# Layernorm scales from a power on GpSimd in place of a square root on ScalarE and a reciprocal on VectorE

## The chip, the cores and the metric

One core of one Trainium2 chip runs the whole kernel in one launch. The metric is device microseconds from the start to the end of the program; less is better. The engines are named as in the profile: PE (TensorE matmul), DVE (VectorE), ACT (ScalarE), POOL (GpSimd), SP (SyncE, which only issues DMAs).

## The reference

The reference is a small transformer of four layers with several kinds of attention and of mixture-of-experts blocks, on 2048 rows (8 x 256) of 256 columns in float32. Each block takes a layernorm of the running sum x and adds its result to x. Cut to what matters:

```python
def _layernorm(x, axis=-1, eps=1e-05):
    m = jnp.mean(x, axis=axis, keepdims=True)
    v = jnp.var(x, axis=axis, keepdims=True)
    return (x - m) / jnp.sqrt(v + eps)

x = x + 0.5 * L0_ffn(_layernorm(x))
x = x + L0_attn(_layernorm(x))
x = x + 0.5 * L0_ffn(_layernorm(x))
x = x + 0.5 * L1_ffn(_layernorm(x))
x = x + L1_attn(_layernorm(x))     # x + its own result; starts with an rms norm
x = x + 0.5 * L1_ffn(_layernorm(x))
x = x + 0.5 * L2_ffn(_layernorm(x))
x = x + L2_attn(_layernorm(x))
x = x + 0.5 * L2_ffn(_layernorm(x))
x = x + 0.5 * L3_ffn(_layernorm(x))
x = x + L3_attn(_layernorm(x))
x = x + 0.5 * L3_ffn(_layernorm(x))
```

Each ffn routes every row to two experts and adds shared experts that every row passes.

## The kernel before

The 2048 rows are 16 tiles (NT) of 128 partitions. x stays on the chip in X (16 tiles of 128x256). The program is a list of thirteen stages, numbered from 0: ffn L0, attn0, ffn L0, moe L1, attn1, ffn AFT (the second half of attn1), moe L1, moe L2, attn2, moe L2, moe L3, attn3, moe L3. Each engine walks through all stages with a program of its own, in the order in which it is written; semaphores join them.

All stages but AFT begin with a layernorm, the "front". It works in four groups of four tiles (GROUP = 4), g = 0 to 3. For each group:

1. DVE takes the moments (front_moments): four bn_stats (L597), four bn_aggr (L600) into MV (mean and variance of each row), and VE = variance + eps (L602). attn1 needs a second scale, since it follows the layernorm with an rms norm: L604 makes its VE, so its tiles are 128x8 instead of 128x4.
2. ACT takes the square root, SD (front_root, L610).
3. DVE takes RS = 1 / SD (L621) and the shift NB = -mean * RS (L622), in front_deviations; attn1 has four operations there (L616 to L619).
4. ACT applies scale and shift, one 128x256 ACTIVATE a tile (front_norm, L631), into XN or XNR. For a moe stage it also issues a DMA that stores the rows to DRAM (front_store, L637), for the experts' gathers.
5. PE transposes the rows (L717), ACT copies the high halves XTH (L723) and DVE takes the low halves XTL (L729): each float32 operand is split into two parts for PE.

In eight stages (0 to 3, 6, 9, 11, 12) the front stands by itself at the start of the stage. In the other four (attn1, the first L2, attn2 and the first L3, stages 4, 7, 8 and 10) it is "tailed": it runs within the tail of the moe stage before it.

The tail of a moe stage brings the experts' results back. POOL issues, tile after tile, two indirect DMAs (the gathers, L1736), one for each of a row's two experts, into YG, whose buffers hold four tiles: the gathers of tile t wait until tile t - 4 is done (x_done). DVE's combines (L1599 and L1604) wait for them and add the weighted rows to X. ACT, PE and DVE go through the tail in numbered slots k: in the slot m.front_of(g) DVE takes the moments of group g, and the square root, the norm, the transposes and the splits of that group follow in this slot and the next three. Tiles 6 and 7 are combined just before the moments of group 0 in an L1 tail, tiles 14 and 15 just before those of group 3.

POOL has other work besides the gathers. At the start of a stage that has weights to split into high and low parts, it casts and subtracts them piece by piece: L2943 and L2945 for the ffn stages and the projections of attn1 and attn3, L1704 and L1706 for the moe stages, L2071 to L2088 for attn0. In a moe stage it also takes some of the shared experts' low halves (SHL, L1573) and issues the gathers of the experts' rows (L1724). Stages 6, 9 and 12 load weights that the program has kept in DRAM from an earlier stage.

PE takes a product with split operands as three matmuls, at L546, L547 and L548. The routing of the ffn and moe stages is a chain of small DVE operations on 128x112 or 128x128 (L756 to L763 for L0).

Of the kernel before, what the change touches and what calls it, by code (L numbers as in the profile page):

```python
# [10 lines left out]
ALU = mybir.AluOpType  # L11
# [151 lines left out]
def build(nc, d, out):  # L163

    with ExitStack() as ctx:
# [44 lines left out]
        M128 = main.put('M128', [P, NT])  # L210
        RST = main.put('RST', [P, 16, NT])
        W12 = main.put('W12', [P, 2, NT])
        SGT = main.put('SGT', [P, NT])
# [353 lines left out]
        def tables_vector(dve):  # L567
# [7 lines left out]
            nc.vector.tensor_copy(HALVES[:, :], MCR[0:32, 3 * P + 2 * NT + 16 * NT:])  # L575
            nc.vector.memset(SEVEN[:, :], 7)
            for m in MOES.values():
                nc.vector.memset(SIZES[:, 2 * m.router:2 * m.router + 1], float(m.ecols))
                nc.vector.memset(SIZES[:, 2 * m.router + 1:2 * m.router + 2], float(m.base))
            nc.vector.memset(RWS[:, :, :, 48:64].bitcast(F32), 0.0)  # L580
            nc.vector.tensor_copy(RWS[:, :, :, 0:16], RWR[:, :, :, :]).then_inc(consts, 1)
            dve.wait_ge(consts, 3)
            nc.vector.tensor_copy(RWS[:, :, :, 32:48], RWR[:, :, :, :])
# [6 lines left out]
        def front_moments(dve, st, g):  # L590
# [8 lines left out]
            for t in tiles:  # L599
                last = nc.vector.bn_aggr(MV[:, t, :], ST6[:, t, :])  # L600
            step(last)
            last = nc.vector.tensor_scalar(VE[:, part], MV[:, part, 1], LN_EPS, None, ALU.add)  # L602
            if st.kind == 'attn1':
                last = nc.vector.tensor_scalar(twice(VE)[:, 1, part], MV[:, part, 1], 1.0 + AFT_EPS, AFT_EPS * LN_EPS, ALU.mult, ALU.add)  # L604
            last.then_inc(ln_var, 1)

        def front_root(act, st, g):
            act.wait_ge(ln_var, GROUPS * st.ln + g + 1)
            sets = slice(0, 1 + (st.kind == 'attn1'))
            nc.scalar.activation(twice(SD)[:, sets, tiles_of(g)[1]], twice(VE)[:, sets, tiles_of(g)[1]], ACT.Sqrt).then_inc(ln_sd, 1)  # L610

        def front_deviations(dve, st, g):
            part = tiles_of(g)[1]
            dve.wait_ge(ln_sd, GROUPS * st.ln + g + 1)
            if st.kind == 'attn1':
                step(nc.vector.reciprocal(twice(RS)[:, :, part], twice(SD)[:, :, part]))  # L616
                step(nc.vector.scalar_tensor_tensor(NB[:, part], MV[:, part, 0], -1.0, twice(RS)[:, 1, part], ALU.mult, ALU.mult))
                nc.vector.scalar_tensor_tensor(MV[:, part, 0], MV[:, part, 0], -1.0, RS[:, part], ALU.mult, ALU.mult)
                nc.vector.tensor_scalar(MV[:, part, 1], RS[:, part], 1.0, None, ALU.add).then_inc(ln_rs, 1)  # L619
                return  # L620
            step(nc.vector.reciprocal(RS[:, part], SD[:, part]))  # L621
            nc.vector.scalar_tensor_tensor(NB[:, part], MV[:, part, 0], -1.0, RS[:, part], ALU.mult, ALU.mult).then_inc(ln_rs, 1)  # L622

# [30 lines left out]
        def front_vector(dve, st):  # L654
            for g in range(GROUPS + 2):
                if g < GROUPS:
                    front_moments(dve, st, g)
                if g == 0 and not st.xd:
                    tables_vector(dve)
                if g >= 2:  # L660
                    front_low(dve, st, 2 * g - 4)
                    front_low(dve, st, 2 * g - 3)
                if g < GROUPS:
                    front_deviations(dve, st, g)
                if g == 1 and st.kind == 'attn0':
                    attn0_prepare(dve, st)

        def front_scalar(act, st):
            for g in range(GROUPS + 2):
                if g < GROUPS:  # L670
                    front_root(act, st, g)
                if 1 <= g < GROUPS + 1:
# [15 lines left out]
        def front_tensor(pe, st):  # L688
            pe.wait_ge(consts, 4)
            for g in range(GROUPS + 2):  # L690
# [700 lines left out]
        def moe_scalar(act, st):  # L1391
# [46 lines left out]
            for k in range(m.front_of(GROUPS - 1) + (4 if nx else 1)):  # L1438
                if k < m.late:
                    shared_scalar(act, st, m.early + k)  # L1440
                for g in range(GROUPS if nx else 0):
# [7 lines left out]
                    if k == done + 1:  # L1449
                        front_norm(act, nx, g)  # L1450
                        if nx.kind == 'moe':
                            front_store(act, nx, g)
                    if k == done:
                        front_root(act, nx, g)
                if nx and nx.kind == 'attn2':
# [150 lines left out]
        def moe_vector(dve, st):  # L1606
# [63 lines left out]
            for k in range(m.front_of(GROUPS - 1) + (3 if nx else 1)):  # L1670
# [3 lines left out]
                for g in range(GROUPS if nx else 0):  # L1674
                    done = m.front_of(g)
                    if k == done + 1:
                        front_deviations(dve, nx, g)
                    if k == done + 2:
# [30 lines left out]
        def moe_pool(pool, st):  # L1709
# [21 lines left out]
            for t in range(NT):  # L1731
                if t >= YGS // 2:
                    pool.wait_ge(x_done, st.xd + t - YGS // 2 + 1)
                for c in range(2):
                    i = 2 * (NT * st.moe + t) + c
                    nc.gpsimd.indirect_dma_start(YG[:, i % YGS, :], None, dyo[0:m.blocks * P, :],  # L1736
                                                 bass.IndirectOffsetOnAxis(ap=POSI[:, c * NT + t:c * NT + t + 1], axis=0)
                                                 ).then_inc(y_in[i // 2 % (YGS // 2)], 16)

        def moe_sync(sp, st):  # L1740
# [324 lines left out]
        def attn0_pool(pool, st):  # L2065
# [15 lines left out]

            rounds = st.pieces // PIECES
            for q in range(PIECES):
                pool.wait_ge(raw_in[q], 16 * (rounds + 1))
                nc.gpsimd.tensor_copy(HWH[:, 0, q * PIECE:(q + 1) * PIECE], RAW[:, q, 0:PIECE]).then_inc(w_hi, 1)
                if q < 2:
                    tap_sums(0, q, 2 * q)
                piece_lo(0, q, st.pieces + q + 1)  # L2088
# [859 lines left out]
        def _(pool):  # L2948
            for st in stages:
                if st.xd and st.kind != 'attn2':  # L2950
                    pool.wait_ge(x_done, st.xd)
                if st.kind == 'moe':
                    moe_pool(pool, st)
# [193 lines left out]
```

## Time and profile before

| | |
|---|---|
| median of three runs | 3247.46 us |
| lowest and highest | 3237.97 and 3249.4 us |
| profiled execution: span, first to last instruction | 3310.2 us |
| PE, DVE, ACT, POOL busy in it | 87%, 67%, 45%, 47% |
| mean clock granted to PE | 0.924 of full |

The profile is of one execution. The only time of its own that it shows is the span, which is 62.7 us above the median of the runs shown. Shares of busy time are means over thirteen stages with different limits: what a change in one place is worth is read from the timeline of that place.

### The profile page before, as it was taken

To read this page: it belongs to the slowest core of one execution; us is meant where nothing else is said; L and a number is where in the kernel's file an instruction comes from. 1 tells how busy PE (TensorE), PEld (TensorE's weight loads), DVE (VectorE), ACT (ScalarE), POOL (GpSimd) and SP (SyncE) were. 2 spreads that over 40 slices of the span, in tenths; PEclk is the share of its full clock that TensorE was granted. 3 is DMA by queue.
4 is the path that set the end of the run, shared out by engine and by line. 5 is a ranking of instruction groups with operands and counts; after the bars stand their busy time and mean duration, and the time that the engine had idled before them with its cause. 6 is when DMAs were issued, how large, how long until landed. Compare 5 with 4: busy or idle time off the path is not lost. (4 is left out here: it accounts for less than half of the span.)

```text
span 3310.2 us, 60075 instructions
## 1 busy us (share of the span) xinstructions
PE 2869.5 (87%) x20922; PEld 2560.7 (77%) x20922; DVE 2213.8 (67%) x5794; ACT 1489.4 (45%) x3235; POOL 1556.3 (47%) x1511
## 2 busy tenths in 40 slices
PE   8979999999999899886897967579997858977798
PEld 6869999999999787774686947557776746956697
DVE  6767777777777677765636656478886555654655
ACT  3356565666566524335323443345444334433342
POOL 2345556555555216444401346658882547350143
PEclk9989999999999898997899977879997869988899
DMA  4022122212121302361005434600003442550533
GB/s 149 1 74 68 53 71 55 71 55 71 55 71 55 114 1 79 103 223 34 20 0 191 122 96 151 205 8 2 2 2 140 118 128 81 193 185 1 204 104 98
DMA packets 147763, 285.78 MB, mean 86 GB/s; under 512 B 20673, under 2 KB 70209, under 8 KB 144385
## 3 DMA queue, kind: packets, MB, share of 16 engines
q1 hardware_dynamic: 113458, 211.38, 19.3%
q0 software_dynamic: 21216, 57.96, 6.6%
q10 hardware_dynamic: 12816, 12.78, 1.1%
q8 instruction: 174, 2.85, 0.4%
q14 instruction: 99, 0.81, 0.1%
HBM read 191.59 MB, written 90.45 MB: 85 GB/s over the span
## 5 line engine op out<-in xcount | busy, mean ns | idle before, releaser
L1724 POOL DMA_INDIRECT MXG<-dxn,IDX x250 | 237.3, 949 | 233.9 <-PE bank L1281 174.3
L1736 POOL DMA_INDIRECT YG<-dyo,POSI x192 | 187.6, 977 | 212.7 <-DMA dyo<-YS 107.7
L2688 POOL TENSOR_SCALAR SX<-SX,MN 128x256 f32<-128x256 f32 x256 | 233.7, 929 | 46.0 <-DVE MN L2619 45.9
L1573 POOL TENSOR_TENSOR SHL<-SGS,SHH 128x512 fp32r<-128x512 f32 x36 | 49.0, 1362 | 425.0 <-ACT SHH L1375 422.8
L2619 DVE CUSTOM_DVE_ANT_0 SX<-bank,FMASK 128x128 f32<-128x128 f32 (+1 forms) x512 | 156.1, 351 | 48.1 <-PE bank L2532 48.0
L1098 POOL TENSOR_TENSOR HL<-HID,HH 128x512 fp32r<-128x512 f32 x56 | 72.4, 1292 | 241.7 <-ACT HH L1063 241.5
L546 PE MATMUL bank<-MWH,GH 128*128 x500 | 171.9, 344 | 13.2 <-DVE HB L1644 6.6
L1411 ACT ACTIVATE GH<-bank 128x256 fp32r<-128x256 f32 x250 | 96.5, 387 | 179.5 <-PE bank L1281 173.6
L546 PE MATMUL bank<-MWH,SHH 128*128 128x256 f32 x352 | 111.7, 317 | 73.6 <-POOL SHL L1573 26.5
L548 PE MATMUL bank<-MWH,GL 128*128 x500 | 156.1, 312 | 0.0
L547 PE MATMUL bank<-MWL,GH 128*128 x500 | 156.0, 312 | 0.0
L1639 DVE TENSOR_TENSOR GL<-bank,GH 128x256 fp32r<-128x256 f32 x250 | 105.5, 423 | 70.9 <-ACT GH L1411 54.1
L2591 ACT ACTIVATE PT<-bank 128x384 f32<-128x384 f32 x256 | 111.7, 490 | 79.9 <-PE bank L2541 79.5
L1988 DVE TENSOR_TENSOR VL<-bank,VH 128x512 fp32r<-128x512 f32 x128 | 82.4, 686 | 96.1 <-ACT VH L1941 96.1
L546 PE MATMUL bank<-MH,XTH 128*128 128x256 f32 x512 | 145.0, 283 | 1.1 <-DVE ML L2036 1.1
L547 PE MATMUL bank<-ML,XTH 128*128 128x256 f32 x512 | 144.9, 283 | 0.0
L548 PE MATMUL bank<-MH,XTL 128*128 128x256 f32 x512 | 144.8, 283 | 0.0
L1418 ACT ACTIVATE HB<-bank 128x176 f32<-128x176 f32 (+1 forms) x250 | 75.7, 303 | 149.3 <-PE bank L548 106.6
L2079 POOL TENSOR_TENSOR HWL<-RAW,HWH 128x640 fp32r<-128x640 f32 x68 | 115.1, 1702 | 56.6 <-DVE DEC L1984 56.4
L546 PEld LDWEIGHTS bank<-MWH,SHH 128*128 128x128 f32 x352 | 73.1, 208 | 88.0 <-issue 30.6
L546 PE MATMUL bank<-MWH,HTH 88*128 (+1 forms) x406 | 136.9, 337 | 1.6 <-DVE HTL L1648 0.9
L546 PE MATMUL bank<-XTH,MWH 128*128 128x512 f32 x320 | 134.4, 420 | 3.8 <-POOL MWL L1706 3.4
(465 smaller groups left out, 11634.0 us busy)
## 6 DMA issues: line engine op xcount, KB each, us to landing
dyo<-YS SPq DMA_DIRECT2D x250, 128.0 KB
RAW<-in_wheads SPq DMA_DIRECT2D x68, 320.0 KB
BB<-dgates SPq DMA_DIRECT2D x68, 256.0 KB, 3.6
GB<-dgates SPq DMA_DIRECT2D x68, 256.0 KB, 4.2
RAW<-in_eL SPq DMA_DIRECT2D x32, 304.0 KB
dkeptL<-MWL SPq DMA_DIRECT2D x32, 304.0 KB
dkeptL<-MWH SPq DMA_DIRECT2D x32, 304.0 KB
MWH<-dkeptL SPq DMA_DIRECT2D x8, 1216.0 KB, 13.3
```

The source lines that it names most:

```text
L546: nc.tensor.matmul(o, lh, rh, start=start, stop=False)
L547: nc.tensor.matmul(o, lh, rl, start=False, stop=False)
L548: return nc.tensor.matmul(o, ll, rh, start=False, stop=stop)
L1411: nc.scalar.activation(GH[:, b % DEEP, :], bank[X_BANK[b % 2]][:, 0:D], ACT.Copy).then_inc(b_xhi, 1)
L1639: nc.vector.tensor_tensor(GL[:, b % DEEP, :], bank[X_BANK[b % 2]][:, 0:D], f32(GH[:, b % DEEP, :]), ALU.subtract).then_inc(b_xlo, 1)
L1724: nc.gpsimd.indirect_dma_start(MXG[:, n % XGS, :], None, dxn, bass.IndirectOffsetOnAxis(ap=IDX[:, b:b + 1], axis=0)).then_inc(x_in[n % XGS ...
L1736: nc.gpsimd.indirect_dma_start(YG[:, i % YGS, :], None, dyo[0:m.blocks * P, :], bass.IndirectOffsetOnAxis(ap=POSI[:, c * NT + t:c * NT + t ...
L1988: return nc.vector.tensor_tensor(VL[:, s % 2, 2 * o:2 * o + 2, :], bank[4 + o][:, :].rearrange('p (t d) -> p t d', t=2), f32(VH[:, s % 2, ...
L2079: nc.gpsimd.tensor_tensor(HWL[:, parity, part], RAW[:, slot, 0:PIECE], f32(HWH[:, parity, part]), ALU.subtract).then_inc(w_ready, 1)
L2591: nc.scalar.activation(PT[:, n % RING3, :], bank[TURNED_IN[n % 2]][:, 0:TRI], ACT.Exp, scale=-1.0).then_inc(s_exp, 1)
L2619: last = nc.vector.tensor_tensor_reduce(out=SX[:, n % RING2, part], in0=o[:, part], in1=FMASK[:, part], scale=-float(HD) ** -0.5, scalar=3 ...
L2688: nc.gpsimd.tensor_scalar(part, part, MN[:, n % RING2, 1:2], None, ALU.subtract).then_inc(s_less1, 1)
```

## The change

The square root on ACT and the reciprocal and products on DVE go. POOL takes one operation for both, a power of VE with the exponent -0.5 out of a new constant tile, MINUS, and then the shift NB as a product with the mean, whose sign DVE now turns in front_moments (one more operation a group). For attn1 POOL takes the four operations. Between the power and the product POOL waits for its own semaphore.

Where POOL does this differs. In the fronts that stand by themselves all four groups come at the start of the stage, before POOL's weight splits; in attn0 the root of group g + 1 stands ahead of piece g of the weights. In the tailed fronts the roots stand in the loop of the gathers: group 0 behind the gathers of tile 7, group 1 behind those of tile 11, groups 2 and 3 behind those of tile 15.

The memset of MINUS raises the semaphore of the constants once more, so the waits on it go from 3 and 4 to 4 and 5, and the roots of stage 0 wait for it too.

```diff
@@ -209,6 +209,7 @@
         IDH = main.put('IDH', [P, NT], F16)
         M128 = main.put('M128', [P, NT])
         RST = main.put('RST', [P, 16, NT])
+        MINUS = main.put('MINUS', [P, 2 * NT])
         W12 = main.put('W12', [P, 2, NT])
         SGT = main.put('SGT', [P, NT])
         POSI = main.put('POSI', [P, 2 * NT], I32)
@@ -574,12 +575,13 @@
             nc.vector.memset(ONE16[:, :], 1.0)
             nc.vector.tensor_copy(HALVES[:, :], MCR[0:32, 3 * P + 2 * NT + 16 * NT:])
             nc.vector.memset(SEVEN[:, :], 7)
+            nc.vector.memset(MINUS[:, :], -0.5).then_inc(consts, 1)
             for m in MOES.values():
                 nc.vector.memset(SIZES[:, 2 * m.router:2 * m.router + 1], float(m.ecols))
                 nc.vector.memset(SIZES[:, 2 * m.router + 1:2 * m.router + 2], float(m.base))
             nc.vector.memset(RWS[:, :, :, 48:64].bitcast(F32), 0.0)
             nc.vector.tensor_copy(RWS[:, :, :, 0:16], RWR[:, :, :, :]).then_inc(consts, 1)
-            dve.wait_ge(consts, 3)
+            dve.wait_ge(consts, 4)
             nc.vector.tensor_copy(RWS[:, :, :, 32:48], RWR[:, :, :, :])
             nc.vector.tensor_tensor(RWS[:, :, :, 16:32], RWR[:, :, :, :], f32(RWS[:, :, :, 0:16]), ALU.subtract).then_inc(consts, 1)
 
@@ -599,27 +601,30 @@
             for t in tiles:
                 last = nc.vector.bn_aggr(MV[:, t, :], ST6[:, t, :])
             step(last)
+            nc.vector.tensor_scalar(MV[:, part, 0], MV[:, part, 0], -1.0, None, ALU.mult)
             last = nc.vector.tensor_scalar(VE[:, part], MV[:, part, 1], LN_EPS, None, ALU.add)
             if st.kind == 'attn1':
                 last = nc.vector.tensor_scalar(twice(VE)[:, 1, part], MV[:, part, 1], 1.0 + AFT_EPS, AFT_EPS * LN_EPS, ALU.mult, ALU.add)
             last.then_inc(ln_var, 1)
 
-        def front_root(act, st, g):
-            act.wait_ge(ln_var, GROUPS * st.ln + g + 1)
+        def front_root(pool, st, g):
+            part = tiles_of(g)[1]
             sets = slice(0, 1 + (st.kind == 'attn1'))
-            nc.scalar.activation(twice(SD)[:, sets, tiles_of(g)[1]], twice(VE)[:, sets, tiles_of(g)[1]], ACT.Sqrt).then_inc(ln_sd, 1)
-
-        def front_deviations(dve, st, g):
-            part = tiles_of(g)[1]
-            dve.wait_ge(ln_sd, GROUPS * st.ln + g + 1)
+            if not st.xd:
+                pool.wait_ge(consts, 5)
+            pool.wait_ge(ln_var, GROUPS * st.ln + g + 1)
+            nc.gpsimd.tensor_tensor(twice(RS)[:, sets, part], twice(VE)[:, sets, part], twice(MINUS)[:, sets, part], ALU.pow).then_inc(ln_sd, 1)
+            pool.wait_ge(ln_sd, GROUPS * st.ln + g + 1)
             if st.kind == 'attn1':
-                step(nc.vector.reciprocal(twice(RS)[:, :, part], twice(SD)[:, :, part]))
-                step(nc.vector.scalar_tensor_tensor(NB[:, part], MV[:, part, 0], -1.0, twice(RS)[:, 1, part], ALU.mult, ALU.mult))
-                nc.vector.scalar_tensor_tensor(MV[:, part, 0], MV[:, part, 0], -1.0, RS[:, part], ALU.mult, ALU.mult)
-                nc.vector.tensor_scalar(MV[:, part, 1], RS[:, part], 1.0, None, ALU.add).then_inc(ln_rs, 1)
+                nc.gpsimd.tensor_tensor(NB[:, part], MV[:, part, 0], twice(RS)[:, 1, part], ALU.mult)
+                nc.gpsimd.tensor_tensor(MV[:, part, 0], MV[:, part, 0], RS[:, part], ALU.mult)
+                nc.gpsimd.tensor_scalar(MV[:, part, 1], RS[:, part], 1.0, None, ALU.add).then_inc(ln_rs, 1)
                 return
-            step(nc.vector.reciprocal(RS[:, part], SD[:, part]))
-            nc.vector.scalar_tensor_tensor(NB[:, part], MV[:, part, 0], -1.0, RS[:, part], ALU.mult, ALU.mult).then_inc(ln_rs, 1)
+            nc.gpsimd.tensor_tensor(NB[:, part], MV[:, part, 0], RS[:, part], ALU.mult).then_inc(ln_rs, 1)
+
+        def front_roots(pool, st):
+            for g in range(GROUPS):
+                front_root(pool, st, g)
 
         def front_norm(act, st, g):
             act.wait_ge(ln_rs, GROUPS * st.ln + g + 1)
@@ -660,15 +665,11 @@
                 if g >= 2:
                     front_low(dve, st, 2 * g - 4)
                     front_low(dve, st, 2 * g - 3)
-                if g < GROUPS:
-                    front_deviations(dve, st, g)
                 if g == 1 and st.kind == 'attn0':
                     attn0_prepare(dve, st)
 
         def front_scalar(act, st):
             for g in range(GROUPS + 2):
-                if g < GROUPS:
-                    front_root(act, st, g)
                 if 1 <= g < GROUPS + 1:
                     front_high(act, st, 2 * g - 2)
                     front_high(act, st, 2 * g - 1)
@@ -686,7 +687,7 @@
                 nc.tensor.matmul(bank[b][:, 0:2 * P], TRB[:, 0, :], TRB[:, :, :].rearrange('p c t -> p (c t)'), start=True, stop=True)
 
         def front_tensor(pe, st):
-            pe.wait_ge(consts, 4)
+            pe.wait_ge(consts, 5)
             for g in range(GROUPS + 2):
                 if st.routed and 2 <= g < GROUPS:
                     moe_logits(pe, st, 2 * g - 4)
@@ -1450,8 +1451,6 @@
                         front_norm(act, nx, g)
                         if nx.kind == 'moe':
                             front_store(act, nx, g)
-                    if k == done:
-                        front_root(act, nx, g)
                 if nx and nx.kind == 'attn2':
                     if k == m.late + 1:
                         act.wait_ge(shared_added, st.added + NW)
@@ -1673,8 +1672,6 @@
                     shared_product(dve, st, m.early + k)
                 for g in range(GROUPS if nx else 0):
                     done = m.front_of(g)
-                    if k == done + 1:
-                        front_deviations(dve, nx, g)
                     if k == done + 2:
                         front_low(dve, nx, 2 * g)
                         front_low(dve, nx, 2 * g + 1)
@@ -1736,6 +1733,9 @@
                     nc.gpsimd.indirect_dma_start(YG[:, i % YGS, :], None, dyo[0:m.blocks * P, :],
                                                  bass.IndirectOffsetOnAxis(ap=POSI[:, c * NT + t:c * NT + t + 1], axis=0)
                                                  ).then_inc(y_in[i // 2 % (YGS // 2)], 16)
+                for g in range(GROUPS if st.next else 0):
+                    if t == min(GROUP * g + GROUP - 1 + YGS // 2, NT - 1):
+                        front_root(pool, st.next, g)
 
         def moe_sync(sp, st):
             m = st.m
@@ -2080,7 +2080,10 @@
                                         ALU.subtract).then_inc(w_ready, 1)
 
             rounds = st.pieces // PIECES
+            front_root(pool, st, 0)
             for q in range(PIECES):
+                if q + 1 < GROUPS:
+                    front_root(pool, st, q + 1)
                 pool.wait_ge(raw_in[q], 16 * (rounds + 1))
                 nc.gpsimd.tensor_copy(HWH[:, 0, q * PIECE:(q + 1) * PIECE], RAW[:, q, 0:PIECE]).then_inc(w_hi, 1)
                 if q < 2:
@@ -2949,6 +2952,8 @@
             for st in stages:
                 if st.xd and st.kind != 'attn2':
                     pool.wait_ge(x_done, st.xd)
+                if st.name != 'AFT' and st.kind != 'attn0' and not st.tailed:
+                    front_roots(pool, st)
                 if st.kind == 'moe':
                     moe_pool(pool, st)
                 if st.kind == 'attn0':
```

## Rows read from the trace of the kernel before

**Rows 1.** The page: busy time of each engine.
```profile
PE 2869.5 (87%) x20922; PEld 2560.7 (77%) x20922; DVE 2213.8 (67%) x5794; ACT 1489.4 (45%) x3235; POOL 1556.3 (47%) x1511
```

**Rows 2.** Groups by line, ACT's and DVE's: count, busy us, mean ns, idle us before, releaser.
```profile
L631 ACT ACTIVATE XN<-X,NB,RS 128x256 f32<-128x256 f32 x128 | 66.2, 590 | 9.3 <-DVE NB L622 9.3
...
L610 ACT ACT_TABLE_LOAD x11 | 14.1, 1283 | 0.9 <-PEq L3139 0.7
...
L610 ACT ACTIVATE SD<-VE 128x4 f32<-128x4 f32 (+1 forms) x48 | 9.6, 201 | 145.2 <-DVE VE L602 98.5 <-issue 34.1 <-DVE VE L604 9.5
...
L621 DVE RECIPROCAL RS<-SD 128x4 f32<-128x4 f32 x44 | 7.7, 176 | 15.6 <-ACT SD L610 13.2 <-issue 2.3
```

**Rows 3.** Groups by line, POOL's.
```profile
L1736 POOL DMA_INDIRECT YG<-dyo,POSI x192 | 187.6, 977 | 212.7 <-DMA dyo<-YS 107.7 <-DVE X L1604 53.4 <-issue 51.6
...
L2680 POOL TENSOR_TENSOR VX<-VF,ONE 128x64 f32<-128x64 f32 x64 | 19.2, 322 | 20.6 <-DVE ONEX L2505 20.6
```

**Rows 4.** Timeline of stage 2's front: start us, us, engine, line [idle before <-releaser].
```profile
1122.24 0.17 DVE L602 TENSOR_SCALAR VE<-MV 128x4 f32<-128x4 f32 x1
...
1123.09 2.08 ACT L631 ACTIVATE XN<-X,NB,RS 128x256 f32<-128x256 f32 x4 [0.45 <-DVE NB L622]
```

**Rows 5.** Timeline of the tail from L1 to attn1 (stages 3 and 4).
```profile
1478.17 0.95 POOL L1736 DMA_INDIRECT YG<-dyo,POSI  x1 [1.69 <-DVE X L1604]
...
1497.30 0.95 POOL L1736 DMA_INDIRECT YG<-dyo,POSI  x1 [0.30 <-issue]
...
1483.20 0.16 DVE L604 TENSOR_SCALAR VE<-MV 128x4 f32<-128x4 f32 x1
...
1505.52 0.87 DVE L1599 SCALAR_TENSOR_TENSOR X<-YG,W,X 128x256 f32<-128x256 f32 x2
...
1509.89 0.16 DVE L604 TENSOR_SCALAR VE<-MV 128x4 f32<-128x4 f32 x1
...
1501.00 2.07 ACT L631 ACTIVATE XNR<-X,NB,RS 128x256 f32<-128x256 f32 x4 [4.42 <-DVE MV L619]
...
1512.67 2.07 ACT L631 ACTIVATE XNR<-X,NB,RS 128x256 f32<-128x256 f32 x4 [2.38 <-DVE MV L619]
...
1517.42 0.77 PE L546 MATMUL bank<-QKVH,XTH 128*128 128x512 f32 x1 [1.50 <-DVE XTL L729]
```

**Rows 6.** Timelines of the other three tails (stages 6 and 7, 7 and 8, 9 and 10).
```profile
1929.12 0.94 POOL L1736 DMA_INDIRECT YG<-dyo,POSI  x1 [1.67 <-DVE X L1604]
...
1934.08 0.17 DVE L602 TENSOR_SCALAR VE<-MV 128x4 f32<-128x4 f32 x1
...
1953.60 2.07 ACT L631 ACTIVATE XNR<-X,NB,RS 128x256 f32<-128x256 f32 x4 [1.04 <-DVE NB L622]
...
2152.63 0.84 ACT L2445 ACTIVATE QKH<-bank,ABIAS 128x256 fp32r<-128x256 f32 x2 [10.74 <-remote]
...
2701.55 0.37 ACT L1203 ACTIVATE LGS<-bank 32x256 f32<-32x256 f32 x1 [5.17 <-remote]
...
2715.01 2.08 ACT L631 ACTIVATE XNR<-X,NB,RS 128x256 f32<-128x256 f32 x4
...
2715.90 1.09 POOL L1736 DMA_INDIRECT YG<-dyo,POSI  x1 [0.30 <-issue]
```

**Rows 7.** Instructions of one line: L602 in stage 3, L602 and L760 in stage 0: ns min/median/max.
```profile
L602 DVE TENSOR_SCALAR VE<-MV x4: 170/443/857, 1290.5 to 1302.9; 128x4 f32<-128x4 f32 x4
...
L602 DVE TENSOR_SCALAR VE<-MV x4: 170/170/855, 6.5 to 18.2; 128x4 f32<-128x4 f32 x4
...
L760 DVE TENSOR_TENSOR RK<-RK,SM x1: 1596/1596/1596, 33.7 to 33.7; 128x112 f32<-128x112 f32 x1
```

**Rows 8.** Timeline of POOL in stages 0 and 3.
```profile
13.65 0.82 POOL L2943 CAST WH<-RAW 128x768 fp32r<-128x768 f32 x1 [13.22 <-DMA RAW<-in_wL]
...
1288.67 0.82 POOL L1704 CAST MWH<-RAW 128x768 fp32r<-128x768 f32 x1 [4.74 <-DVEq L1133]
...
1337.30 1.28 POOL L1573 TENSOR_TENSOR SHL<-SGS,SHH 128x512 fp32r<-128x512 f32 x1 [4.72 <-ACT SHH L1375]
```

## Prediction

> **What bounds the kernel now.** I read the page's busy times first: PE is busy for 87% of the span of 3310.2 us, DVE for 67%, ACT and POOL for under half [rows 1]. No engine that the change relieves is the bound, so the change can only count where one of the twelve layernorms ("fronts") stands on the chain. Then the groups by line, to see what the old path costs: 48 square roots of 0.2 us on ACT, each followed by a reciprocal of 0.18 us on DVE. DVE stood idle for the root 13.2 us in all, ACT for the shift (NB) before XN 9.3 us in all [rows 2]. The ACT row's 98.5 us of idle time before SD is time in which ACT waited for the variance, which stays. So whatever the new path saves, the old path's waits put about 22 us on it as a ceiling.
>
> Next the timeline of one front with nothing else going on: from the start of VE to the start of XN are 0.85 us [rows 4]. Last, the timelines of the four fronts that run in the tail of a mixture-of-experts stage, with POOL's rows beside DVE's, because there the new POOL work stands in a program that already has 32 gathers of some 0.95 us to issue, one each 1.25 us [rows 3, 5].
>
> The profiled execution's span is 62.7 us above the median of the three runs (3247.46). I make the sum as differences within the profiled execution and add it to the median.
>
> **The change, part by part.**
>
> *The price of the root.* A power is not in the trace of before. From below: a plain operation on the same 128x4 tile, 0.17 us (on DVE) [rows 4]. From above: an indirect gather on POOL, 0.98 us for a list of 128 addresses [rows 3]. I take 0.4 us, near the 128x64 two-input row (0.322 us), which handles 16 times the elements of a 128x4 root: it allows about 16 plain operations for each power. A plain root then is 0.4, about 0.1 for the wait on its own semaphore, and 0.19 for the product NB: 0.7 us; attn1's, with three operations behind it, 1.1 us.
>
> The Trainium skill (GPSIMD Engine Reference, 2.1 Instruction dispatch) says that the first call of newly loaded GpSimd code costs about 6 us that no instruction shows; no run here shows that for a power. By it the sum would be +25 instead of +19, as an estimate from that page, still inside the range.
>
> *Fronts in the open.* VE to XN was 0.85 us [rows 4]; now it is 0.17 + 0.08 (the new sign flip ahead of it) + 0.7 + two handovers of 0.1: about 1.1 us, +0.3 for the first group of a front. The other groups are hidden: DVE no longer stands for SD and runs ahead, and ACT had only 9.3 us of waits for NB in 128 XN [rows 2]. Eight fronts: between -2 and +2 us; I take -1, with attn0's half microsecond of gain in it (its second half had waited for DVE). If the cover of ACT and PE's transposes were gone, each group would cost 0.3 us, 10 us over 32 groups.
>
> *Table loads.* Eleven loads of 1.28 us go, and attn1's own square root needs one again. The loads' row has 0.9 us of idle time before it, and the ACT instruction behind it waited 98.5 us in all for VE [rows 2]: they are hidden behind that wait. I take +0.6 for the new one in attn1.
> The Trainium skill (ScalarE: Activation LUTs, What ACT_TABLE_LOAD costs) prices a switch at 2.66 us with its drain; were all eleven on the path, that would be an estimated 29 us of gain and turn the sum into -10. The trace disagrees, as said.
>
> *The tails.* POOL's program now holds the root of group 0 between the gathers of tiles 7 and 8, that of group 1 behind tile 11's, those of groups 2 and 3 behind tile 15's. What is queued behind root 0: sixteen gathers; DVE's combines wait for these, and the next moments and roots for the combines.
>
> L1 to attn1 [rows 5]: gather 8 went at 1478.17. Root 0 can't start until VE ends, 1483.36, and takes 1.1: gather 8 now goes at about 1484.5, +6.3. The sixteen run without a gap in both, so the last one ends not at 1498.25 but at about 1505.7, with root 1 (1.1) between. Root 2 stands behind it: XNR of group 2 at about 1507.0 instead of 1501.00, +6. DVE's low halves and the combine of tiles 14 and 15 (1505.52) move with it to 1511.5, VE of group 3 from 1510.05 to 1515.5. There 2 us come back: before, 2.6 us passed from that to XNR (1512.67), because POOL was splitting the projection's weights and DVE's small operations were stretched; now the splits stand behind root 3, and it takes 1.3: XNR at 1516.8, +4.1. The splits (5.3 us for two pieces) then end at about 1522, against PE's first product at 1517.42 + 4.1 = 1521.5: +0.6. Together +4.7.
>
> L1 to L2 [rows 6]: gather 8 went at 1929.12; VE ended at 1934.25, so it now goes at 1935.05, +5.9. Sixteen gathers and root 1 end at 1956.2, root 2 at 1956.9, XNR of group 2 at 1957.1 instead of 1953.60. +3.5, and the same for group 3.
>
> L2 to attn2 [rows 6]: root 0 waits for POOL (+3.8), but every engine then stood still until 2152.63, ACT for 10.7 us. What comes early or late before that is swallowed: +0.3.
>
> L2 to L3 [rows 6]: the last gather ends at 2716.85, because its buffer came free late; root 2 behind it, XNR of group 2 at 2717.9 instead of 2715.01: +2.9.
>
> Tails together: 4.7 + 3.5 + 0.3 + 2.9 = 11.4. If such idle times, which no instruction of the kernel explains (10.7 us here, 5.2 in the next tail, and smaller ones [rows 6]), are the profile's alone, the full holds count instead, about 6.5 us for each of the last three in place of 6.7 together: +24.
>
> *Weight splits at stages 0 and 3.* The four roots stand before POOL's splits. In stage 3 the last VE starts at 1302.9; without contention (below) it would be at about 1299, so the splits start at 1299.8 11 us later than the 1288.67 of before [rows 8]. They ended at 1332.6, 4.7 us before POOL's first shared low half (SHL, 1337.30) [rows 8], for which PE's product waits; now that starts some 6 us late. And the contention moves: small DVE operations are stretched while POOL works on the same memory (VE up to 0.86 against 0.17 us, and 1.60 us for the routing's L760 [rows 7]). It leaves the front (-1.7) and falls on ten more operations of the routing at some 0.7 each (+7). Net +5, between -2 (the late half hidden, the front's gain kept) and +9.
> Stage 0: the last VE starts at 18.2, so the splits start at about 18.4 to 18.9 instead of 13.65, some 5 us late [rows 7, 8]; they cover five to nine more routing operations: +3, between 0 and +5.
>
> *Sum*: -1 + 0.6 + 11.4 + 5 + 3 = +19, and 3247.5 + 19 = 3266.5.
>
> **Rivals.**
>
> *No change (a).* The idle times in the tails end together with POOL's gathers. If something of the gathers causes them, holding gathers only moves them, and the holds and the idle times overlap in all four tails; then -1 + 0.6 + 3 for stage 0 and nothing for stage 3, where PE has other work to take first: +2.6, 3250. Speaks for it: ACT idle 10.7 us to 2152.63. Against: in the first tail the chain from gather 8 to XNR is closed by semaphores.
>
> *Faster (b).* An unbroken run of gathers is what stalls the other engines, and the roots break it up. If the two large idle times go (-16), and with them the holds that they swallow or cause (11.4 falls to 5), while the rest costs its +7.6: -3 and, with half of the 22 us of old waits given back on the chain (-11), -14: 3233. It decides from the point where the idle time of the tails falls by more than the holds' 11. Against: the roots hold a run for 6 us and do not shorten it.
>
> *Slow power (c).* If a power goes element by element and costs 2 us, each tail is longer by about three roots (two behind the last gather), 4 x 5, and each first group in the open by 1.6 x 8 = 13: +19 + 20 + 13 = +52, 3299. At 0.98 us, the upper row, it is about +31, 3278.
>
> *Holds in full (d).* The idle times are not in unprofiled runs: 19 - 11.4 + 24 = +32, 3279.
>
> **How the numbers follow.** My forecast has 0.47, (a) 0.18, (b) 0.14, (c) 0.07, (d) 0.14. A measurement of this kernel can tell about 0.5%, 16 us, from no change. The forecast's own range, by the bounds of stages 0 and 3, the root's price and the tails, is 3252 to 3281, so about a third of its 0.47 falls within 0.5%: 0.15, and with 0.17 of (a) same has 0.32. Faster: (b) 0.14 and a little of (a), 0.15. Slower: the rest, 0.53. The range leaves out the far ends of (b) and (c): 3234 to 3292. The time is that of the forecast.
>
> **What the profile after would show.** Power rows of 0.3 to 0.5 us on POOL; gather 8 of each tail behind the root of group 0, its idle time put to VE; 1.25 us between the later gathers as before; stage 3's splits ending near 1343 with its start as now, and its first POOL SHL without idle time before it; routing rows of stages 0 and 3 stretched for longer, the fronts' VE at 0.17. It would be wrong by a root of another price, by idle times in the tails that change, or if PE has work to cover the later splits.

## The result and the profile after

The changed kernel takes 3319.11 us (median of 4 runs, 3313.68 to 3325.62) against 3242.72 before: a ratio of 1.0234, 95% interval 1.0219 to 1.0248, so 76 us slower. The forecast was 3266.5 with a range to 3292: the direction was right, the size was off by 53 us.

The page of the changed kernel shows nearly the same busy shares as before [rows 1], with POOL at 49% instead of 47%; nothing in it says that 76 us were lost. Its span is 3311.9 us against the 3310.2 of the profiled execution of before, so these two pages side by side show no loss at all.

```profile
PE 2872.5 (87%) x20922; PEld 2561.0 (77%) x20922; DVE 2206.8 (67%) x5739; ACT 1477.5 (45%) x3177; POOL 1620.4 (49%) x1615
```

Its groups by line on POOL price the root (the columns are those of [rows 3]):

```profile
L1733 POOL DMA_INDIRECT YG<-dyo,POSI x192 | 187.1, 975 | 178.9 <-DMA dyo<-YS 104.6 <-issue 48.3 <-DVE X L1603 26.0
...
L616 POOL TENSOR_TENSOR RS<-VE,MINUS 128x4 f32<-128x4 f32 (+1 forms) x48 | 51.6, 1075 | 347.9 <-DVE VE L605 322.7 <-DVE VE L607 15.5 <-DVE RWS L586 9.5
...
L623 POOL TENSOR_TENSOR NB<-MV,RS 128x4 f32<-128x4 f32 x44 | 8.9, 203 | 3.5
```

The power costs 1.075 us on average: 1.02 for 128x4 and 1.68 for attn1's 128x8. The prediction took 0.4 for it, with an upper bound of 0.98. The product is 0.20, as expected.

A front in the open, the same as in [rows 4], in the timeline of the changed kernel:

```profile
1126.46 0.16 DVE L605 TENSOR_SCALAR VE<-MV 128x4 f32<-128x4 f32 x1
...
1126.77 1.02 POOL L616 TENSOR_TENSOR RS<-VE,MINUS 128x4 f32<-128x4 f32 x1 [12.32 <-DVE VE L605]
1127.86 0.20 POOL L623 TENSOR_TENSOR NB<-MV,RS 128x4 f32<-128x4 f32 x1
...
1128.10 2.08 ACT L636 ACTIVATE XN<-X,NB,RS 128x256 f32<-128x256 f32 x4 [9.64 <-POOL NB L623]
...
1131.87 2.06 ACT L636 ACTIVATE XN<-X,NB,RS 128x256 f32<-128x256 f32 x4
```

From VE to XN are now 1.64 us instead of 0.85. The second group's XN follows 3.77 us behind the first, as before: in this front only the first group pays.

**The tails.** First the kernel before, profiled once more (the first experiment below), in the tail from L1 to attn1:

```profile
1475.38 0.95 POOL L1736 DMA_INDIRECT YG<-dyo,POSI  x1 [1.40 <-DVE X L1604]
...
1494.57 1.02 POOL L1736 DMA_INDIRECT YG<-dyo,POSI  x1 [0.30 <-issue]
...
1481.80 2.07 ACT L631 ACTIVATE XNR<-X,NB,RS 128x256 f32<-128x256 f32 x4 [0.74 <-DVE MV L619]
...
1494.42 2.08 ACT L631 ACTIVATE XNR<-X,NB,RS 128x256 f32<-128x256 f32 x4 [1.45 <-DVE MV L619]
...
1506.09 2.08 ACT L631 ACTIVATE XNR<-X,NB,RS 128x256 f32<-128x256 f32 x4 [2.38 <-DVE MV L619]
...
2124.98 0.84 ACT L2445 ACTIVATE QKH<-bank,ABIAS 128x256 fp32r<-128x256 f32 x2 [0.71 <-PE bank L548]
```

Gather 8 (1475.38) goes before the variance of group 0 is there, the last gather ends at 1495.6, and from group 0's XNR to group 3's are 24.3 us. The last line is ACT in the tail from L2 to attn2: where the rows ahead of the prediction have 10.74 us of idle time [rows 6], it has 0.71.

The same tail of the changed kernel:

```profile
1495.38 1.67 POOL L616 TENSOR_TENSOR RS<-VE,MINUS 128x8 f32<-128x8 f32 x1 [6.96 <-DVE VE L607]
...
1498.01 1.09 POOL L1733 DMA_INDIRECT YG<-dyo,POSI  x1 [0.19 <-issue]
...
1508.12 1.68 POOL L616 TENSOR_TENSOR RS<-VE,MINUS 128x8 f32<-128x8 f32 x1
...
1520.47 0.95 POOL L1733 DMA_INDIRECT YG<-dyo,POSI  x1 [0.30 <-issue]
1521.44 1.68 POOL L616 TENSOR_TENSOR RS<-VE,MINUS 128x8 f32<-128x8 f32 x1
...
1532.24 1.67 POOL L616 TENSOR_TENSOR RS<-VE,MINUS 128x8 f32<-128x8 f32 x1 [8.49 <-DVE VE L607]
...
1513.11 0.17 DVE L607 TENSOR_SCALAR VE<-MV 128x4 f32<-128x4 f32 x1
...
1497.85 2.07 ACT L636 ACTIVATE XNR<-X,NB,RS 128x256 f32<-128x256 f32 x4 [10.79 <-POOL MV L621]
...
1523.78 2.08 ACT L636 ACTIVATE XNR<-X,NB,RS 128x256 f32<-128x256 f32 x4 [8.70 <-POOL MV L621]
...
1534.57 2.08 ACT L636 ACTIVATE XNR<-X,NB,RS 128x256 f32<-128x256 f32 x4 [6.91 <-POOL MV L621]
...
1528.30 0.87 DVE L1598 SCALAR_TENSOR_TENSOR X<-YG,W,X 128x256 f32<-128x256 f32 x2
```

Root 0 stands with 6.96 us of idle time, put to VE: POOL has issued the gathers of tiles 0 to 7 and waits for the variance, and gather 8 (1498.01) waits behind the root. Root 1 (1508.12) has no idle time of its own: the variance was there, and what it costs is its own 1.68 us and three small operations. Root 2 (1521.44) starts when the last gather has gone; its variance had been ready since 1513.28, the end of L607. So XNR of group 2 comes 25.9 us after group 0's, where it took 12.6 before, and the combine of tiles 14 and 15 (1528.30) follows it. From group 0 to group 3 are 36.7 us: 12.4 more.

The same difference, from the start of the first XNR of group 0 to that of group 3, in the four tails (us, each worked out from two timeline rows):

```
                        attn1   L2 (stage 7)   attn2   L3 (stage 10)   sum
before, rows 5 and 6     28.3       28.0        41.7       39.8       137.8
before, profiled again   24.3       21.9        31.5       31.5       109.2
changed                  36.7       33.4        38.0       34.0       142.2
```

These spans leave out what comes before group 0's XNR. From the start of the tail's first gather to the start of group 3's XNR are:

```
                        attn1   L2 (stage 7)   attn2   L3 (stage 10)   sum
before, rows 5 and 6     60.0       61.6        59.9       55.5       237.1
before, profiled again   54.7       51.4        49.9       47.1       203.1
changed                  69.0       63.9        61.4       55.7       249.9
```

So the four tails lose 46.8 us in these executions, and 13.9 of them come before the first XNR, 11.0 in the two tails behind an L2 stage (to attn2 and to L3). There it is the root that waits for the gathers ahead of it in POOL's program, and not the gathers for the root. This is the tail from L2 to attn2, first XNR of group 0 in the kernel before, profiled again, then the changed kernel:

```profile
2113.25 2.08 ACT L631 ACTIVATE XNR<-X,NB,RS 128x256 f32<-128x256 f32 x4 [0.44 <-DVE NB L622]
...
2158.10 0.23 DVE L605 TENSOR_SCALAR VE<-MV 128x4 f32<-128x4 f32 x1
...
2162.23 1.05 POOL L616 TENSOR_TENSOR RS<-VE,MINUS 128x4 f32<-128x4 f32 x1
...
2163.60 2.08 ACT L636 ACTIVATE XNR<-X,NB,RS 128x256 f32<-128x256 f32 x4 [22.20 <-POOL NB L623]
```

The variance is there at 2158.33, the root comes 3.9 us later without idle time of POOL, behind the gathers up to tile 7, and ACT stands for it.

**Stages 3 and 0.** Timeline of POOL and PE in stage 3 of the changed kernel, to be read against [rows 8]:

```profile
1306.88 1.01 POOL L616 TENSOR_TENSOR RS<-VE,MINUS 128x4 f32<-128x4 f32 x1 [2.79 <-DVE VE L605]
...
1308.10 0.82 POOL L1701 CAST MWH<-RAW 128x768 fp32r<-128x768 f32 x1
...
1353.16 1.57 POOL L1572 TENSOR_TENSOR SHL<-SGS,SHH 128x512 fp32r<-128x512 f32 x1
...
1354.79 0.58 PE L547 MATMUL bank<-MWH,SHH 128*128 128x256 f32 x1 [6.00 <-POOL SHL L1572]
```

The last of the four roots (1306.88) waits for its variance; the splits start behind it, at 1308.10, and end 45 us later; POOL's first SHL follows them without idle time, and PE waits 6.00 us for it. In stage 0 the routing's operations are the long ones. Its line L759 (L758 before) stands twice in the routing, first on RK, then on CB:

```profile
L759 DVE TENSOR_TENSOR RK<-RK,ORD x1: 1906/1906/1906, 33.6 to 33.6; 128x112 f32<-128x112 f32 x1
L759 DVE TENSOR_TENSOR CB<-CB,ORD x1: 1847/1847/1847, 39.0 to 39.0; 128x112 f32<-128x112 f32 x1
```

Before, in the run profiled again, the two took 0.78 and 0.28 us: the second set of the routing now runs while POOL still splits weights.

### The profile page after: what moved, and what is told of

Same layout as the page of the kernel before. It is cut to its first block and busy times, and to the rows that moved or that the text cites. A ratio compares the mean times of both kernels' runs of the same rounds, so it can differ in the third digit from the quotient of the medians.

```text
span 3311.9 us, 60073 instructions
## 1 busy us (share of the span) xinstructions
PE 2872.5 (87%) x20922; PEld 2561.0 (77%) x20922; DVE 2206.8 (67%) x5739; ACT 1477.5 (45%) x3177; POOL 1620.4 (49%) x1615
## 5 line engine op out<-in xcount | busy, mean ns | idle before, releaser
L616 POOL TENSOR_TENSOR RS<-VE,MINUS 128x4 f32<-128x4 f32 (+1 forms) x48 | 51.6, 1075 | 347.9 <-DVE VE L605 322.7
L730 DVE TENSOR_TENSOR XTL<-bank,XTH 128x512 fp32r<-128x512 f32 x104 | 68.8, 688 | 110.1 <-ACT XTH L724 109.3
L2114 POOL TENSOR_TENSOR QL<-QG,QH 128x512 fp32r<-128x512 f32 x64 | 83.0, 1297 | 106.3 <-ACT QH L1908 106.3
```

## The experiments

Times are medians, but for the first line, which is one run. The ratio is to the kernel before on the same chip, with its 95% interval. The runs come from several chips, so where a median and a ratio tell slightly different differences, both are given.

```
                                               us    ratio   interval
before, again                              3249.6
changed                                    3319.1   1.0234   1.0219 to 1.0248
power in the eight open fronts only        3271.5   1.0102   1.0080 to 1.0124
power in the four tails only               3295.8   1.0176   1.0149 to 1.0202
power in stages 0 and 3 only               3264.0   1.0055   1.0035 to 1.0074
power in the six calm open fronts only     3261.4   1.0040   1.0027 to 1.0054
changed, power made a product              3283.6   1.0134   1.0112 to 1.0156
changed, roots retimed in the tails        3296.7   1.0156   1.0133 to 1.0179
changed, group 2's root retimed alone      3308.1   1.0194   1.0172 to 1.0217
changed, roots woven in stages 0 and 3     3305.8   1.0184   1.0160 to 1.0208
changed, retimed and woven                 3287.4   1.0136   1.0110 to 1.0161
changed, retimed, woven, product           3254.1   1.0033   1.0020 to 1.0046
```

**Is the idle time of the tails the kernel's?** The kernel before, unchanged, was profiled once more.

> The kernel before, unchanged, profiled once more. Theory H (the holds in the tails count in full, because the idle times without a releaser belong to the one profiled execution): the span is near 3245 us and the idle times put to 'remote' (10.7 us on ACT at the tail from L2 to attn2, 5.2 and 4.9 in the tail from L2 to L3) are gone. Rival I (the idle times belong to the kernel and the change removed them): the span is near 3310 us again, with more than 20 us of such idle time.

Its span is 3247.7 us, one run took 3249.6, and the idle times are gone (the last line of the first tail timeline above). They belonged to the one execution on which the prediction rests: none of the twelve other profiles, of this kernel or a changed one, has any idle time put to 'remote'.

**Where the loss is.** Each front either takes the power on POOL or keeps the old path; the added test, with its two settings:

```diff
+        def by_pool(st):
+            return not st.tailed        # the open fronts only
+            return st.tailed            # the tails only
...
         def front_root(pool, st, g):
+            if not by_pool(st):
+                return
```

> The power on POOL in the eight fronts that stand by themselves; the four tailed fronts keep ACT's square root and DVE's reciprocal. Theory H (most of the 76 us is lost in the tails, where gathers stand behind a root): about 20 us slower than before, 3255 to 3270. Rival F (most is lost in the open fronts and behind the later weight splits of stages 0 and 3): 45 us or more slower, above 3288.

> The power on POOL in the four tailed fronts alone; the eight others keep ACT's square root and DVE's reciprocal. Theory H: about 55 us slower than before, 3290 to 3308, so some 14 us a tail. Rival F: 30 us or less slower, below 3273. If the two halves add up, this and the run with the open fronts alone together lose about 76 us.

The open fronts cost 1.02%, 33 us, and the tails 1.76%, 57 us (48 to 65); the timeline of the second run shows 46.6 of them between the first gathers and group 3's XNR, as in the changed kernel. Together the two are 90 against 76. The difference of 14 us is at the edge of what the intervals allow, so that the two halves simply add up is not shown. The tails lead, as theory H has it; the open fronts cost more than its 20 us.

Then the open fronts were parted in two:

```diff
+        def by_pool(st):
+            return (not st.tailed and not st.cached and (st.kind == 'moe' or st.name == 'L0'))  # stages 0 and 3
+            return not st.tailed and not (not st.tailed and not st.cached and (st.kind == 'moe' or st.name == 'L0'))  # the six others
```

> The power on POOL only in the fronts of stages 0 and 3, all four roots before the weight splits, as in the changed kernel; all others as before. Theory S: about 17 to 28 us slower than before, nearly all of what the eight open fronts together lost (32 us). Rival: 10 us or less slower, so that the loss of the open fronts is spread over all eight.

> The power on POOL only in the six open fronts with no gathers and no split of stage 0 or 3 behind it (attn0, the second ffn L0, the second L1, L2 and L3 and attn3); all others as before. Theory H (a front in the open hides the root behind ACT and PE's transposes but for its first group, 0.7 us each with a power of 1.01 us, and attn0 gains 1): 0 to 6 us slower than before. Rival G (the removed root, reciprocal and table loads are a gain where nothing stands behind the root): 5 us or more faster than before. Rival F (every group pays): 20 us slower.

Stages 0 and 3 cost 18 us, within the 17 to 28 of theory S, but not nearly all of the loss: the six others cost 13, more than the 0 to 6 of theory H, less than the 20 of rival F, and no gain as rival G has it. First groups explain a part of the six: from the first moments operation (L597) of a front to its first XN are 2.71 us before and 3.57 to 3.61 here, so 6 x 0.9 = 5 us. From there to the front's last XN the six together are no longer than before, so their other groups do hide the root. The other 8 us have an interval of 4 us to either side and no place of their own in the timelines, whose stages differ by some us from one execution to the next; they stay open.

**What the power costs.** The power becomes a product of two constant tiles of the same shapes (MINUS holds 0.3 here); scale and output are not the reference's. The routing of rows to experts differs with the values, but the page counts as many instructions on PE, DVE, ACT and POOL as for the changed kernel.

```diff
-nc.gpsimd.tensor_tensor(twice(RS)[:, sets, part], twice(VE)[:, sets, part], twice(MINUS)[:, sets, part], ALU.pow).then_inc(ln_sd, 1)
+nc.gpsimd.tensor_tensor(twice(RS)[:, sets, part], twice(MINUS)[:, sets, part], twice(MINUS)[:, sets, part], ALU.mult).then_inc(ln_sd, 1)
```

> The changed kernel with the power replaced by a plain product of two constant tiles of the same shapes, at the same places and behind the same waits: the scale is a constant, so the values are not the reference's. The product is expected at 0.2 us for 128x4 instead of the power's 1.01. Theory H (the wait for the variance and the place in POOL's program count, the power's price little): three roots a tail and the first root of each open front are on the path, some 18 us less than the changed kernel, 3295 to 3305. Rival P (the price of the power is the cause): 40 us or more less, below 3280.

The group on POOL in that run:

```profile
L616 POOL TENSOR_TENSOR RS<-MINUS 128x4 f32<-128x4 f32 (+1 forms) x48 | 9.6, 200 | 361.3 <-DVE VE L605 335.2 <-DVE VE L607 16.5 <-DVE RWS L586 9.4
```

It takes 0.20 us instead of 1.075, and the whole is 32 us faster by the ratios (1.0234 to 1.0134), 35 by the medians. The rows of the two runs differ by 42 us in busy time (51.6 to 9.6), so most of it is on the path. That lies between the two theories and nearer to the rival's 40: theory H had too little for the price. In the four tails the second sum above falls from 249.9 to 232.4 by it, so 29 us of loss stay there with a cheap root.

**Where POOL's program has the roots in the tails.**

```diff
-                    if t == min(GROUP * g + GROUP - 1 + YGS // 2, NT - 1):
+                    if t == ((9, 11, 13, 15) if m.gated else (5, 9, 13, 15))[g]:
                         front_root(pool, st.next, g)
```

> The changed kernel with its roots at other places among the gathers of the four tails: behind the gathers of tiles 9, 11 and 13 in an L1 tail, 5, 9 and 13 in an L2 tail (the last stays behind tile 15's), where the variance is there when POOL comes by. The power and the number of roots stay. Theory W (POOL waits in its queue for the variance, and groups 2 and 3 stand behind the last gather, and that holds the gathers): the four tails lose about 20 us instead of 33, and the whole is 10 to 16 us faster than the changed kernel, 3300 to 3309. Rival R (the roots' own time among gathers that follow each other without a gap is the loss, wherever they stand): within 5 us of the changed kernel, 3313 to 3324.

This is 22 us faster than the changed kernel by the medians and 25 by the ratios, more than the 10 to 16 of theory W; the rival is out. From the first gather to group 3's XNR the four tails take 227.9 us here instead of 249.9, which is those 22 us; theory W had counted from group 0's XNR alone. The tail from L1 to attn1 in that run's timeline, POOL and then ACT:

```profile
1507.99 1.68 POOL L616 TENSOR_TENSOR RS<-VE,MINUS 128x8 f32<-128x8 f32 x1
...
1510.91 1.11 POOL L1733 DMA_INDIRECT YG<-dyo,POSI  x1 [0.18 <-issue]
...
1515.80 1.68 POOL L616 TENSOR_TENSOR RS<-VE,MINUS 128x8 f32<-128x8 f32 x1
...
1522.61 0.95 POOL L1733 DMA_INDIRECT YG<-dyo,POSI  x1 [0.30 <-issue]
...
1502.96 2.07 ACT L636 ACTIVATE XNR<-X,NB,RS 128x256 f32<-128x256 f32 x4 [11.20 <-POOL MV L621]
...
1518.56 2.08 ACT L636 ACTIVATE XNR<-X,NB,RS 128x256 f32<-128x256 f32 x4 [3.91 <-POOL MV L621]
...
1531.31 2.07 ACT L636 ACTIVATE XNR<-X,NB,RS 128x256 f32<-128x256 f32 x4 [8.87 <-POOL MV L621]
```

Roots 1 and 2 (1507.99, 1515.80) have no idle time, and XNR of group 2 comes 15.6 us after group 0's instead of 25.9. Between two pairs of gathers there still are 3 us of root: from group 0's XNR to group 3's are 28.3 us, against 24.3 before.

One root alone was then moved:

```diff
-                    if t == min(GROUP * g + GROUP - 1 + YGS // 2, NT - 1):
+                    if t == (7, 11, 13, 15)[g]:
```

> The changed kernel with one root a tail moved: that of group 2 behind the gathers of tile 13 instead of behind tile 15's. Theory Q (in the L1 tails group 2's place behind the last gather costs 6.2 and 4.7 us, as much as the wait before gather 8): 6 to 12 us faster than the changed kernel, 3307 to 3313. Rival (only the wait of POOL for group 0 before gather 8 counts): 3315 or more.

It is 11 us faster by the medians and 13 by the ratios: group 2's place behind the last gather is about half of what retiming wins. The rest is, by the difference, put to the places of groups 0 and 1, which were not moved by themselves.

**Where POOL's program has the roots in stages 0 and 3.** A root of stage 3 comes before pieces 1, 2, 4 and 5, of stage 0 before pieces 0, 0, 1 and 2, and the four at the start of these two stages go:

```diff
+        def weave(pool, st, j):
+            for g in range(GROUPS):
+                if woven(st) and j == ((1, 2, 4, 5) if st.kind == 'moe' else (0, 0, 1, 2))[g]:
+                    front_root(pool, st, g)
```

> The changed kernel with the roots of stages 0 and 3 woven between the weight pieces (stage 3: before pieces 1, 2, 4 and 5; stage 0: before pieces 0, 0, 1 and 2) instead of all four before the first piece. Theory S (the late start of the splits costs stages 0 and 3 about 6 and 10 us): 8 to 13 us faster than the changed kernel, 3304 to 3312. Rival (it is the roots' latency in the front, not the splits): no faster, 3315 or more.

It is 13 us faster by the medians, 16 by the ratios: all roots ahead of the splits cost that. POOL and PE at the same place as in stage 3 above:

```profile
1348.46 1.26 POOL L1580 TENSOR_TENSOR SHL<-SGS,SHH 128x512 fp32r<-128x512 f32 x1
...
1349.78 0.39 PE L547 MATMUL bank<-MWH,SHH 128*128 128x256 f32 x1 [1.58 <-POOL SHL L1580]
```

SHL still follows the splits without idle time, but PE waits 1.58 us for it instead of 6.00.

**Both moves, and the rest.**

> The changed kernel with both moves: roots retimed among the gathers of the tails (9, 11, 13, 15 in L1 tails, 5, 9, 13, 15 in L2 tails) and woven between the weight pieces of stages 0 and 3. Theory A (two separate causes that add up: 22 us of holds in the tails, 14 to 16 us of late splits): 3277 to 3287, some 37 us faster than the changed kernel and still 35 to 42 us slower than before. Rival (they share their time): no better than the better of the two alone, 3293 or more.

This is 32 us faster than the changed kernel, 0.4 us above theory A's range: the two moves add up within their intervals. With the product in place of the power in addition (values not the reference's):

> Both moves, and the power replaced by a product of two constant tiles (0.2 us instead of 1.01; values not the reference's). Theory A says that what both moves leave is the power's own time, on the path nearly everywhere (35 us less when it was made cheap without the moves): 3246 to 3258, within 0.5% of before. Rival (a rest has another cause, such as POOL's two more handovers a group): 3262 or more.

This wins 33 us more and ends 0.33% above before, as theory A has it. So of the 76 us about 32 are the places of the roots, 33 the price of the power, and 11 (6 to 15) a rest. In the timelines 7.5 us of that rest lie in the four tails (210.6 against 203.1 from the first gather to group 3's XNR, one execution each); no run tells its cause.

No run was faster than the kernel before.

## Why the prediction was wrong

**The tails: the step that failed.** The prediction took differences against one profiled execution and let its idle times swallow the holds ("What comes early or late before that is swallowed: +0.3"). From the first gather to group 3's XNR the four tails took 237.1 us there and 203.1 when profiled again; the changed kernel takes 249.9. So the loss is 47 us (57 by the run with the tails alone), where the sum had 11.4; tail by tail it is 14.3, 12.5, 11.4 and 8.5 where the sum had 4.7, 3.5, 0.3 and 2.9. In the L1 tails the holds came as described: gather 8 waits for root 0, with 6.96 us of idle time before it, and root 2 stands behind the last gather. In the tail from L2 to attn2 the wait of root 0 for POOL had been seen (+3.8) and then been put at nothing; in the one from L2 to L3 it was not in the sum. Retiming the roots won 22 us. Rivals (a) and (b) both build on idle times that the kernel profiled again does not have. Rival (d), which let the holds count in full, had the right mechanism: its 24 us are near the 29 that the tails lose with the cheap root, and the power's price makes up the other 18. The warning was in the table: a span 62.7 us above the median of the runs. (One reading was off without effect: by its row the last gather of the tail from L2 to L3 ended at 2716.99, not 2716.85.)

**The price of the root.** It was taken at 0.4 us from a row of plain operations, and measured at 1.02 and 1.68; a whole root takes 1.3 us instead of 0.7, and attn1's 2.4 instead of 1.1. The upper bound was nearly the value for 128x4, and no row told that a tile of twice the columns costs more. Making the power cheap won 32 to 35 us in the changed kernel and 33 after the moves. That is rival (c)'s direction, at half the price that it named. Its count, three roots a tail and one in each open front, was too small: by it, 0.87 us less for a power would have won some 18 us. Even (c) at 0.98 us and (d) together would have come to +44.

**Stages 0 and 3.** The mechanism held as written: roots first, splits late, the first SHL without idle time, routing operations stretched for longer. Forecast were 8 us together; alone they cost 18 (11 to 24), and in the changed kernel the woven version gives back 13 to 16. In stage 3 the splits did start some 11 us later than before, measured from the front's XN; by the timelines the stage lost 6.7 us by it from its group 3's XN to its first gather (146.6 to 153.3, and 146.7 when woven), near the 5 of the sum. Stage 0 lost 6.3 from its group 3's XN to attn0's first (160.1 to 166.4, and 163.1 when woven), of which 0.9 is attn0's own first group; the sum had 3 for it. How much of this is PE's wait and how much the stretched routing was not parted.

**Fronts in the open.** The sum had -1 for all eight; the six away from stages 0 and 3 cost 13. Their first groups pay 0.9 us each, because of the power's price, which is 5 of it, and attn0's gain of half a microsecond did not come with the power at this price. That the other groups hide the root was right within the fronts: XN follows XN in 3.77 us. The other 8 us have no cause that a run shows.

**Table loads.** The eleven loads of L610 went, one came at the start of the program and one more in attn1, as forecast there. No run takes the loads alone, but none with the power on POOL gained anything, which agrees with the reading that they were hidden. Where the Trainium skill (GPSIMD Engine Reference, 2.1 Instruction dispatch) has some 6 us for the first call of newly loaded code, no run here shows it for the power: stage 0's first XN came 1.45 us later than in the run of before profiled again, and the root's 1.0 us in place of ACT's 0.2 is in that.

## What to carry to other kernels

Compare the profiled execution's span with the runs' median before taking a difference from it; idle time without a releaser in an execution that is 2% too long is no cover for anything. An operation put into another engine's program can wait for its input and hold all that is queued behind it, or be ready and wait for what is queued ahead: ask for each place whether its input is there when the engine comes by. An operation whose price no row shows deserves the far bound in the sum when it stands 48 times in the program.

## What the runs showed of the hardware

The power on GpSimd took 1.02 us for 128x4 and 1.68 for 128x8, where a product took 0.20 for either. Between two indirect gathers it started without a gap, and the gather behind it went 0.2 us after the last small operation. A 128x112 DVE operation of 0.28 us took 1.85 to 1.91 while GpSimd was splitting weights, longer than the 1.60 that the rows of before had shown.
